# Cross-attention and mixture-of-experts block in one kernel: experts chosen first, two of four routers as VectorE dots, and the first pair of feed-forward slices in another order

## The chip, the core and the metric

The kernel runs on one core of one Trainium2 chip. The metric is the time of one execution on the device, in microseconds (us). The engines are named as in the profile: PE is TensorE's matmul (PEld its weight load), DVE is VectorE, ACT is ScalarE, POOL is GpSimd, SP is SyncE, which only issues DMAs here.

## The reference, cut to what matters

```python
x = x + xattn(layernorm(x), gate_up, ctx)        # int8-like quantised linear, silu gate, linear
x = x + ffn(layernorm(x), gate_w, w1, b1, w2, b2)

def ffn(hidden, gate_w, w1, b1, w2, b2):         # 2048 tokens, 512 wide, 8 experts, top 2
    router_logits = x @ gate_w.T                                   # [2048, 8]
    _, sel = top_k(router_logits.sum(axis=0), 2)                   # two experts for ALL tokens
    rw = softmax(router_logits[:, sel], axis=1)                    # [2048, 2]
    h = gelu(einsum('nd,kdf->knf', x, w1[sel]) + b1[sel])          # f = 2048
    y = einsum('knf,kfd->knd', h, w2[sel]) + b2[sel]
    return einsum('nk,knd->nd', rw, y)
```

The same two experts serve every token. Which two they are depends only on the sum of the logits over the tokens. The softmax over two values needs only the difference of the two logits of a token.

## The kernel before, in words

Four batches of 512 tokens are held in SBUF. The first part (the quantised layers and the second layer norm) has an order written out by hand for each engine; it ends near 140 us. The normalised tokens are transposed on PE (`normed2`), copied out by ACT and DVE, and split into a high part (`keep_hi`, ACT) and a low part (`keep_lo(b, h)`, DVE: full value minus high part), b being the batch and h one half of the 512 features. Every fp32 product is then three matmuls: high with high, high with low, low with high.

The expert choice is short: `token_sums` and `token_total` (DVE) sum the tokens, `expert_sums` (PE, four tiny matmuls) multiplies by the gate weights, `choose_experts` (DVE) takes the two largest, and SP then issues the DMAs of the chosen experts' weights (`load_w1`, `load_w2`) by register. The per-token logits come from `router(b)`: eight matmuls for each batch, an ACT copy (`keep_logits`), small transposes (`logit_columns`), and on DVE `pick_logits`; POOL takes a power (`lpow`), and `token_weights` on DVE makes the softmax weights `rw`.

The feed-forward work goes over 16 pairs p (two experts, eight slices of 256 hidden units), each in two token halves tp (batches 0 and 1, then 2 and 3). Pair 0 is done plainly: four up tiles (`plain`, 12 matmuls each), then `down` (48 matmuls), twice. From pair 1 on the up product is done by a seven-product scheme (`strassen`, 42 matmuls) over sums of operands: `last_operands`, `middle_operands`, `fourth_operand` and `operand_lo` on DVE and `operand_hi` on ACT make those sums during pair 0 and pair 1. DVE also adds every down product to the result (`outputs_of`, four instructions for each quarter; each frees one bank for PE by `y_free`), adds the bias rows (`bias_rows`) and makes the combinations `combine(e2...)` that the fourth and the later products of a pair wait for. GELU is on ACT (`gelu`), its low part on POOL (`hid_lo`), and so are the sums and low parts of the next weights (`weight_sums`, `weight_lo`, `down_lo`).

Each engine runs its own list of instructions in the written order and waits on semaphores; nothing is reordered by a scheduler. The names above are functions of kernel.py. Lines of the profile: L1291 `keep_lo`, L1295 `difference` (last and middle operands), L1310 `fourth_operand`, L1316 `operand_lo`, L1361 to L1368 `pick_logits`, L1519 to L1523 `token_weights`, L1532 `bias_rows`, L1541 `outputs_of`, L1570 `combine`, L656 `normed2`, L667 `router`, L677 `expert_sums`, L685 `logit_columns`, L850 `plain`, L805 `down`, L792 `strassen`, L340 `inv_std`, L476 `hid_lo`, L523 the power of the softmax.

Of the kernel before, what the change touches and what calls it, by code (L numbers as in the profile page):

```python
# [5 lines left out]
ALU = mybir.AluOpType  # L6
# [17 lines left out]
def xattn_ffn(  # L24
# [21 lines left out]
    NT = B * TT  # L46
    FW = 2 * P
# [14 lines left out]
    with ExitStack() as ctx:  # L62
# [6 lines left out]
        def each(name):  # L69
# [42 lines left out]
        logits = sb("logits", [2 * E, B, T])  # L112
# [8 lines left out]
        lk = sb("lk", [P, TOPK, NT])  # L121
        lmin = sb("lmin", [P, NT])
        lmax = sb("lmax", [P, NT])
# [12 lines left out]


# [16 lines left out]
        rstd = [batch_sb(f"rstd{c}_", [P, TT]) for c in (1, 2)]  # L154
        nmean = [batch_sb(f"nmean{c}_", [P, TT]) for c in (1, 2)]
# [78 lines left out]
        raw1_load, raw2_load = sem("raw1_load"), sem("raw2_load")  # L234
        b1_load, b2_load = sem("b1_load"), sem("b2_load")
# [18 lines left out]
        def _(sp):  # L254
# [63 lines left out]
        def _(pool):  # L318
# [200 lines left out]
            def first_pair():  # L519
                hid_lo(0, 0, 0)  # L520
                hid_lo(0, 0, 1)
                pool.wait_ge(lsub_ready, 1)
                g.tensor_tensor(lpow[:, :], euler[:, :], lsub[:, :], ALU.pow).then_inc(lexp_ready, 1)  # L523
                hid_lo(0, 0, 2)
                hid_lo(0, 0, 3)
                weight_sums(0)
                for i in range(4):
                    hid_lo(0, 1, i)
                for i in range(7):
                    weight_lo(0, i)  # L530
                down_lo(0, 0, 1)
                down_lo(0, 1, 0)

            first_pair()
# [6 lines left out]
        def _(pe):  # L541
# [139 lines left out]
            def logit_columns(b):  # L681
                emptied(f"r.{b}")
# [156 lines left out]
            def plain(q, n):  # L839
# [3 lines left out]
                for h in range(KD // H):  # L843
                    if q == 0:
                        pe.wait_ge(a_ops_ready, 2 * f + h + 1)
                    pe.wait_ge(lo_ready[b], h + 1)
                    hi, lo = HI_AT[s][h], LO_AT[s][h]
                    for k in range(H):
                        for a, v in ((a_hi, hi), (a_hi, lo), (a_lo, hi)):
# [5 lines left out]
            def first_pair():  # L855
                for tp in range(2):
                    pe.wait_ge(hid_ready, 8 + 8 * tp)
                    if tp == 0:
                        pe.wait_ge(drained[0], ALL_DRAINED[0])
                    plain(tp, 0)  # L860
                    plain(tp, 1)
                    if tp == 0:
                        pe.wait_ge(drained[1], ALL_DRAINED[1])
                        for b in range(B):
                            logit_columns(b)
                    plain(tp, 2)
                    pe.wait_ge(hid_ready, 8 + 8 * tp + 2)
                    plain(tp, 3)
                    if tp == 0:
                        pe.wait_ge(w2_ready, 2)  # L870
                        pe.wait_ge(drained[2], ALL_DRAINED[2])
                        pe.wait_ge(drained[3], ALL_DRAINED[3])
                    down(0, tp, 0, 0, 0, True)
                    down(0, tp, 0, 1, 1, False)
                    last = down(0, tp, 1, 2, 1, True)
                    if tp == 1:
                        last.then_inc(w2_free, 1)
                    down(0, tp, 1, 3, 0, False)
                pe.wait_ge(hid_ready, 8 + 16)

            first_pair()
# [7 lines left out]
        def _(act):  # L889
# [107 lines left out]
            def first_weights(lo, hi):  # L997
                if lo == 0:
                    act.sem_inc(hid_ready, 8)
                    act.sem_inc(e1_ready, 2)  # L1000
                    act.wait_ge(raw1_load, 16)
                for i in range(lo, hi):
                    plain_hi(i)
# [82 lines left out]
            keep_summed(2, 1)  # L1086
            keep_hi(2, 0)
            keep_hi(2, 1)
            keep_summed(3, 1)
            keep_hi(3, 0)  # L1090
            keep_hi(3, 1)
            keep_logits(0)
            keep_logits(1)
            first_weights(0, 2)
            first_weights(2, 4)
            s.activation(gelu_warm[:, :], half[:, 0:1], ACT.Gelu_apprx_tanh)
            keep_logits(2)
            keep_logits(3)
            first_down_weights()
# [6 lines left out]
            def first_pair():  # L1106
                act.wait_ge(b1_ready, 1)
                s.copy(b1_now[:, :], b1_col[:, 0:2]).then_inc(b1_ready, 1)
                act.wait_ge(b1_ready, 2)
                for tp in range(2):  # L1110
                    act.wait_ge(h_ready, 4 + 4 * tp)
                    for n in range(4):
                        act.wait_ge(prod_done, 7 * tp + n + 1)
                        gelu(0, n, TILES[n][0], TILE_BANK[n])
                    if tp == 0:
                        operand_hi(0, (T2H, T2L), 4)
                        operand_hi(0, (T3H, T3L), 4)
                        operand_hi(0, (T1H, T1L), 4)
                        operand_hi(0, (T4H, T4L), 4)
# [55 lines left out]
            first_pair()  # L1175
# [7 lines left out]
        def _(dve):  # L1183
# [172 lines left out]

            def pick_logits():
                dve.wait_ge(logcol_ps, B)
                cols = bank[3][:, 0:2 * NT * E].rearrange("p (n e) -> p n e", e=2 * E)
                for k in range(TOPK):  # L1360
                    link(v.tensor_tensor(picked[:, :, :], cols,  # L1361
                                         onehot[:, k:k + 1, :].to_broadcast([P, NT, 2 * E]), ALU.mult))
                    link(v.tensor_reduce(lk[:, k, :], picked[:, :, :], AX.X, ALU.add))
                v.tensor_tensor(lmin[:, :], lk[:, 0, :], lk[:, 1, :], ALU.min)
                link(v.tensor_tensor(lmax[:, :], lk[:, 0, :], lk[:, 1, :], ALU.max))
                v.tensor_tensor(lsub[:, :], lmin[:, :], lmax[:, :], ALU.subtract).then_inc(lsub_ready, 1)
                v.tensor_tensor(is_top[:, 0, :], lk[:, 0, :], lk[:, 1, :], ALU.is_ge)
                link(v.tensor_tensor(is_top[:, 1, :], lk[:, 1, :], lk[:, 0, :], ALU.is_ge))  # L1368
# [135 lines left out]
            choose_experts()  # L1504
            keep_lo(2, 0)
            keep_lo(2, 1)
            keep_lo(3, 0)
            keep_lo(3, 1)
            first_weights(0, 2)
            first_weights(2, 4)  # L1510
            pick_experts()
            pick_bias()
            first_down_weights()
# [112 lines left out]
```

## Time and profile before

| what | value |
|---|---|
| time, median of 3 runs | 821.65 us (820.04 to 822.15) |
| span of the profiled execution | 818.7 us |
| median of the runs less this span | 2.95 us |
| PE busy | 771.5 us, 94% of the span |
| DVE busy | 477.7 us, 58% |
| ACT busy | 354.6 us, 43% |
| POOL busy | 449.7 us, 55% |

The profile gives the span of its own execution and no time of its own around it; the median of the three runs stands 2.95 us above the span. A row of a timeline tells when an engine started an instruction, how long it was busy with it, what it reads and writes, and in brackets how long the engine was idle before it and who ended that. Instructions of one kind are merged (x4); a merged row's time runs from the first start to the last end. From about 154 us on PE is busy without a break but for fractions of a microsecond.

### The profile page before, as it was taken

To read this page: it belongs to the slowest core of one execution; us is meant where nothing else is said; L and a number is where in the kernel's file an instruction comes from. 1 tells how busy PE (TensorE), PEld (TensorE's weight loads), DVE (VectorE), ACT (ScalarE), POOL (GpSimd) and SP (SyncE) were. 2 spreads that over 40 slices of the span, in tenths; PEclk is the share of its full clock that TensorE was granted. 3 is DMA by queue.
4 is the path that set the end of the run, shared out by engine and by line. 5 is a ranking of instruction groups with operands and counts; after the bars stand their busy time and mean duration, and the time that the engine had idled before them with its cause. 6 is when DMAs were issued, how large, how long until landed. Compare 5 with 4: busy or idle time off the path is not lost.

```text
span 818.7 us, 11342 instructions
## 1 busy us (share of the span) xinstructions
PE 771.5 (94%) x3570; PEld 624.1 (76%) x3577; DVE 477.7 (58%) x669; ACT 354.6 (43%) x660; POOL 449.7 (55%) x497
## 2 busy tenths in 40 slices
PE   5688666999999999999999999999999999999998
PEld 4666455688788888888888888888888888888886
DVE  5999759797754545454545454545454545454545
ACT  3967588743442434343424343434343434242422
POOL 1789997157564646464646464646464646464622
PEclk9899968999999999999999999999999999999999
DMA  9400000301010101010101010101010101010022
GB/s 344 173 2 1 1 0 2 129 1 51 1 52 1 51 0 49 3 50 2 48 4 51 1 45 6 42 9 44 7 41 11 36 15 36 15 32 19 0 103 104
DMA packets 19077, 32.34 MB, mean 39 GB/s; under 512 B 872, under 2 KB 11240, under 8 KB 18160
## 3 DMA queue, kind: packets, MB, share of 16 engines
q1 hardware_dynamic: 18896, 31.98, 11.1%
q8 instruction: 12, 0.20, 0.1%
q10 hardware_dynamic: 160, 0.08, 0.0%
q14 instruction: 9, 0.07, 0.0%
HBM read 27.87 MB, written 4.19 MB: 39 GB/s over the span
## 4 chain that ended last, share of the span: by engine, by line
PE 83%; POOL 8%; DVE 3%; issue 2%; ACT 2%; DMA 1%; ACTq 0%; POOLq 0%; DVEq 0%
PE slot L805 42%; PE slot L792 34%; PE slot L850 3%; POOL wv L366 2%; POOL xf L383 1%; PE slot L667 1%; POOL wv L372 1%; POOL cv L366 1%; PE slot L585 1%; DVE rmax L1226 1%; DMA b_rows<-in_L_ffn_b 1%; POOL rstd L340 1%; POOL h_lo L476 1%; DVE stats L1217 1%; DVE peak_x L1226 1%
## 5 line engine op out<-in xcount | busy, mean ns | idle before, releaser
L792 PE MATMUL slot<-xo,a_hi 128*128 128x512 f32 x840 | 259.1, 390 | 0.0
L1541 DVE SCALAR_TENSOR_TENSOR res<-slot,rw,res 128x512 f32<-128x512 f32 x256 | 178.5, 750 | 130.3 <-PE slot L805 130.2
L1570 DVE TENSOR_TENSOR e<-slot,e 128x512 f32<-128x512 f32 x150 | 103.8, 692 | 173.4 <-PE slot L792 173.3
L805 PE MATMUL slot<-w_hi,h_hi 128*128 128x512 f32 x512 | 201.3, 393 | 0.4 <-POOL h_lo L476 0.4
L805 PE MATMUL slot<-w_lo,h_hi 128*128 128x512 f32 x512 | 199.6, 390 | 0.0
L805 PE MATMUL slot<-w_hi,h_lo 128*128 128x512 f32 x512 | 199.4, 390 | 0.0
L792 PEld LDWEIGHTS slot<-xo,a_hi 128*128 128x128 f32 x840 | 157.4, 188 | 33.3 <-DVE e L1570 0.2
L476 POOL TENSOR_TENSOR h_lo<-e,h_hi 128x512 fp32r<-128x512 f32 x96 | 138.1, 1451 | 55.0 <-ACT e L1104 54.0
L792 PE MATMUL slot<-xo,a_lo 128*128 128x512 f32 x420 | 163.7, 390 | 0.0
L805 PEld LDWEIGHTS slot<-w_hi,h_hi 128*128 128x128 f32 x512 | 96.1, 188 | 25.1 <-POOL h_lo L476 5.6
L476 POOL TENSOR_TENSOR h_lo<-hid,h_hi 128x512 fp32r<-128x512 f32 x32 | 44.1, 1378 | 124.7 <-ACT hid L1104 124.7
L805 PEld LDWEIGHTS slot<-w_hi,h_lo 128*128 128x128 f32 x512 | 96.2, 188 | 20.1
L805 PEld LDWEIGHTS slot<-w_lo,h_hi 128*128 128x128 f32 x512 | 96.2, 188 | 19.3
L792 PEld LDWEIGHTS slot<-xo,a_lo 128*128 128x128 f32 x420 | 78.9, 188 | 16.5
L1103 ACT ACTIVATE h_hi<-e,b_now 128x512 fp32r<-128x512 f32 x90 | 64.9, 721 | 58.0 <-DVE e L1570 57.6
L1142 ACT COPY e<-slot 128x512 f32<-128x512 f32 x30 | 17.6, 587 | 164.5 <-PE slot L792 164.5
L490 POOL TENSOR_TENSOR a_lo<-raw,a_hi 128x256 fp32r<-128x256 f32 x45 | 34.3, 761 | 95.9 <-ACT a_hi L988 95.9
L991 ACT CAST w_hi<-raw 128x512 fp32r<-128x512 f32 x32 | 19.8, 622 | 109.8 <-PE slot L805 109.8
L495 POOL TENSOR_TENSOR w_lo<-raw,w_hi 128x512 fp32r<-128x512 f32 x30 | 38.7, 1289 | 50.4 <-ACT w_hi L991 50.4
L1104 ACT ACTIVATE e<-e,b_now 128x512 f32<-128x512 f32 x90 | 63.8, 709 | 0.0
L1103 ACT ACTIVATE h_hi<-slot,b_now 128x512 fp32r<-128x512 f32 x38 | 26.2, 689 | 66.5 <-PE slot L792 56.6
L490 POOL TENSOR_TENSOR a_lo<-ssum,a_hi 128x256 fp32r<-128x256 f32 x60 | 43.7, 739 | 0.0
(145 smaller groups left out, 814.5 us busy)
## 6 DMA issues: line engine op xcount, KB each, us to landing
raw<-in_L_ffn_w SPq DMA_DIRECT2D x32, 512.0 KB, 3.4
res<-in_x SPq DMA_DIRECT2D x4, 1024.0 KB, 11.9
wv<-in_fside_BxS2xS SPq DMA_DIRECT2D x4, 1024.0 KB, 12.8
out_x<-res SPq DMA_DIRECT2D x3, 1024.0 KB, 3.9
cv<-in_ctx SPq DMA_DIRECT2D x4, 512.0 KB, 13.1
out_x<-res SPq DMA_DIRECT2D x4, 256.0 KB, 2.7
b_row<-in_L_ffn_b SPq DMA_DIRECT2D x2, 256.0 KB, 4.6
b_rows<-in_L_ffn_b ACTq DMA_DIRECT2D x1, 64.0 KB, 6.0
```

Of the source, the lines that this page charges most:

```text
L366: g.tensor_tensor(w[:, j, :], w[:, j, :], rows[b][:, 0:n], ALU.mult).then_inc(wmul_ready[b], 1)
L476: g.tensor_tensor(h_lo[:, i, :], hid[i][:, :], h_hi[:, i, :].bitcast(F32), ALU.subtract).then_inc(h_ready, 1)
L490: g.tensor_tensor(a_lo[:, i, :, :], A_OF[i], a_hi[:, i, :, :].bitcast(F32), ALU.subtract).then_inc(a_ops_ready, 1)
L495: g.tensor_tensor(w2_lo[:, f, :], raw2[:, f, :], w2_hi[:, f, :].bitcast(F32), ALU.subtract).then_inc(w2_ready, 1)
L792: last = t.matmul(dst, a[:, i, k, :], xo[tp][:, v, k, :], start=(start and n == 0), stop=(n == 3 * H - 1), skip_group_check=True)
L805: last = t.matmul(y_bank[j][:, :], a[:, i, j * P:(j + 1) * P], v[:, f, :], start=(start and n == 0), stop=(not start and n == 2), skip_gro ...
L850: last = t.matmul(TILE_BANK[n], a[:, 2 * f + h, k, :], xo[q][:, v, k, :], start=(m == 0), stop=(m == 3 * KD - 1))
L991: s.copy(w2_hi[:, f, :], raw2[:, f, :]).then_inc(w2_hi_ready, 1)
L1103: s.activation(h_hi[:, i, :], src, ACT.Gelu_apprx_tanh, bias=bias).then_inc(hid_ready, 1)
L1104: s.activation(hid[i][:, :], src, ACT.Gelu_apprx_tanh, bias=bias).then_inc(hid_ready, 1)
L1541: v.scalar_tensor_tensor(out=r, in0=y_bank[j][:, :], scalar=rw[:, ds(p, 1), n:n + 1].rearrange("p a b -> p (a b)"), in1=r, op0=ALU.mult, o ...
L1570: v.tensor_tensor(dst[:, :], src, other[:, :], ALU.add).then_inc(comb_ready, 1)
```

## The change

- The two experts' choice comes ahead of everything that can wait: on DVE `keep_lo(0, 0)` and `keep_lo(0, 1)` go behind `choose_experts`, and `expert_sums` goes ahead of both routers on PE.
- Only `router(1)` and `router(0)` stay on PE. The logit differences of batches 2 and 3 are computed on DVE by `router_dots(2)` and `router_dots(3)`: eight instructions over 128x512 with a running sum, of the tokens in SBUF and of the difference of the two gate rows, which SP loads by two DMAs more and POOL subtracts (`gate_difference`). They stand behind the outputs of the first token half.
- The softmax is done in two halves of eight columns; the denominator's `+ 1` moves to POOL (`token_power`).
- The first weight tile is loaded by two DMAs, and the first up tile starts with products of the high part alone.
- `keep_lo` of batches 2 and 3, the GELUs and the operand passes are written in another order. DVE makes the low parts of the down weights (`first_down_weights`) ahead of `keep_lo(3, 0)`, `token_weights(0)` and `keep_lo(3, 1)`.

VectorE's order behind the choice of the experts, before (`xo<-xf,xo` at L1291 is `keep_lo`, `w_lo` the down weights' low parts, `lk` the picked logits, `xf<-xf` at L1295 the operand sums):

```order
L1349 MAX_INDEX top_i<-top_v,sum_row 128x8
L1291 TENSOR_TENSOR xo<-xf,xo 128x1024 x4
L1381 TENSOR_TENSOR a_lo<-raw,a_hi 128x256 x4
L1353 CAST top_f<-top_i 128x8
...
L1388 TENSOR_TENSOR w_lo<-raw,w_hi 128x512 x2
L1361 TENSOR_TENSOR picked<-slot,onehot 128x256
...
L1295 TENSOR_TENSOR xf<-xf 128x1024 x2
```

And now, the same stretch of VectorE (`xo<-xf,xo` at L1333 is `keep_lo`, `lsub` at L1424 the logit maxima, L1574 and on the token weights):

```order
L1391 MAX_INDEX top_i<-top_v,sum_row 128x8
L1333 TENSOR_TENSOR xo<-xf,xo 128x1024 x2
L1395 CAST top_f<-top_i 128x8
...
L1438 TENSOR_TENSOR a_lo<-raw,a_hi 128x256 x4
L1333 TENSOR_TENSOR xo<-xf,xo 128x1024
L1415 TENSOR_TENSOR between<-onehot 128x16
...
L1424 SCALAR_TENSOR_TENSOR lsub<-ldiff 128x8
L1333 TENSOR_TENSOR xo<-xf,xo 128x1024
L1445 TENSOR_TENSOR w_lo<-raw,w_hi 128x512 x2
L1333 TENSOR_TENSOR xo<-xf,xo 128x1024
L1574 TENSOR_TENSOR lexp<-lpow,is_top 128x2x8
...
L1333 TENSOR_TENSOR xo<-xf,xo 128x1024
```

Six `keep_lo` passes now stand between the choice and the first operand sums, where four stood.

VectorE between the first outputs and pair 1's first combination, before (`res<-slot,rw,res` is a quarter of the outputs, L1316 `operand_lo`, L1532 the bias rows, `e<-slot,e` the first combination):

```order
L1541 SCALAR_TENSOR_TENSOR res<-slot,rw,res 128x512 x4
L1316 TENSOR_TENSOR xo<-xf,xo 128x1024 x4
L1295 TENSOR_TENSOR xf<-xf 128x1024 x2
L1310 TENSOR_TENSOR xf<-xf 128x1024
L1532 SCALAR_TENSOR_TENSOR res<-b_row,rw,res 128x512 x2
L1541 SCALAR_TENSOR_TENSOR res<-slot,rw,res 128x512 x8
L1570 TENSOR_TENSOR e<-slot,e 128x512
```

The same stretch now:

```order
L1597 SCALAR_TENSOR_TENSOR res<-slot,rw,res 128x512 x4
L1337 TENSOR_TENSOR xf<-xf 128x1024
L1405 SCALAR_TENSOR_TENSOR xf,ldot<-res,late_nmean,gate_row 128x512 x4
L1409 TENSOR_TENSOR ldiff<-ldot,late_rstd 128x4
...
L1424 SCALAR_TENSOR_TENSOR lsub<-ldiff 128x8
L1358 TENSOR_TENSOR xo<-xf,xo 128x1024 x3
L1574 TENSOR_TENSOR lexp<-lpow,is_top 128x2x8
...
L1588 SCALAR_TENSOR_TENSOR res<-b_row,rw,res 128x512 x2
L1610 TENSOR_TENSOR e<-slot,e 128x512
```

The eight dots and a second set of token weights have come in ahead of the second half's outputs, and the bias rows stand last ahead of the combination.

The diff, cut to its core:

```diff
@@ sync @@
-            load_w1(0)
+            sp.dma_start(raw1[:, 0:H, :], first[:, 0:H, :]).then_inc(raw1_top, 16)
+            sp.dma_start(raw1[:, H:KD, :], first[:, H:KD, :]).then_inc(raw1_load, 16)
             load_w2(0)
             expert.append(value_of(1))
+            for k in range(TOPK):
+                sp.dma_start(gate_row[:, k, :], gate_w[ds(expert[k], 1), :].to_broadcast([P, D])).then_inc(gate_load, 16)
@@ gpsimd @@
+            def token_power(tp):
+                pool.wait_ge(lsub_ready, tp + 1)
...
+                link(g.tensor_tensor(lpow[:, at], euler[:, at], lsub[:, at], ALU.pow))
+                g.tensor_scalar(lden[:, at], lpow[:, at], 1.0, None, ALU.add).then_inc(lexp_ready, 1)
+            hid_lo(0, 0, 0)
+            token_power(0)
+            hid_lo(0, 0, 1)
+            hid_lo(0, 0, 2)
+            hid_lo(0, 0, 3)
+            gate_difference()
+            weight_sums(0)
+            hid_lo(0, 1, 0)
+            hid_lo(0, 1, 1)
+            token_power(1)
...
@@ tensor @@
+            expert_sums()
             router(1)
-            expert_sums()
             router(0)
-            router(2)
-            router(3)
...
+            up_tile(0, 0)
+            logit_columns(1)
+            logit_columns(0)
+            up_tile(0, 1)
+            up_tile(0, 2)
+            up_tile(0, 3)
+            first_downs(0)
@@ vector @@
+            def router_dots(b):
...
+                for j in range(TT):
...
+                    ins = v.scalar_tensor_tensor(out=product, in0=res[:, n, :], scalar=nmean[1][b][:, j:j + 1],
+                                                 in1=gate_row[:, 0, :], op0=ALU.add, op1=ALU.mult,
+                                                 accum_out=ldot[:, n:n + 1])
+                link(ins)
+                link(v.tensor_tensor(ldiff[:, b * TT:b * TT + TT], ldot[:, b * TT:b * TT + TT], rstd[1][b][:, :],
+                                     ALU.mult))
...
-            keep_lo(0, 0)
+            normalise_last()
             keep_lo(1, 0)
-            normalise_last()
             token_sums(2)
-            keep_lo(1, 1)
             token_sums(3)
             token_total()
+            keep_lo(1, 1)
+            choose_experts()
+            keep_lo(0, 0)
             keep_lo(0, 1)
...
+            outputs_of(0, 0, 1)
+            middle_operands(0, 4)
+            router_dots(2)
+            router_dots(3)
+            logit_maxima(1)
+            operand_lo(0, 0)
+            operand_lo(0, 1)
+            operand_lo(0, 2)
+            token_weights(1)
+            outputs_of(0, 1, 0)
+            operand_lo(0, 3)
+            last_operands(1)
+            outputs_of(0, 1, 1)
+            fourth_operand(1)
...
+            bias_rows(0)
             pair(1, True, False)
```

## Rows read from the trace of the kernel before

**Rows 1.** The page's chain that ended last: shares by engine.

```profile
PE 83%; POOL 8%; DVE 3%; issue 2%; ACT 2%; DMA 1%; ACTq 0%; POOLq 0%; DVEq 0%
```

**Rows 2.** Timeline of PE: start us, us, instruction, idle before and its releaser.

```profile
143.41 3.14 PE L667 MATMUL slot<-xo,gwt 128*16 128x512 f32 x8
146.38 0.95 PE L677 MATMUL slot<-gwt_full,tok_total 128*128 128x8 f32 x8
147.19 6.52 PE L667 MATMUL slot<-xo,gwt 128*16 128x512 f32 x24
153.55 0.62 PE L850 MATMUL slot<-xo,a_hi 128*128 128x512 f32 x2
159.11 1.17 PE L685 MATMUL slot<-ident,logits 16*128 16x16 f32 x16
...
165.81 0.39 PE L805 MATMUL slot<-w_hi,h_hi 128*128 128x512 f32 x1
...
198.44 0.62 PE L792 MATMUL slot<-xo,a_hi 128*128 128x512 f32 x2
```

**Rows 3.** Stretches: us, PE, PEld, DVE, ACT, POOL busy, PEclk, DMA share, GB/s.

```profile
144.00:146.00 2.00, 2.00 (x7) 0.70 (x6) 1.87 (x3) 2.00 (x3) 0.00 (x0) 0.58 0.00 0
146.00:148.00 2.00, 2.00 (x15) 1.38 (x14) 1.01 (x6) 2.00 (x4) 0.00 (x0) 1.00 0.00 0
148.00:201.36 53.36, 53.15 (x243) 41.15 (x241) 45.24 (x63) 24.99 (x46) 29.67 (x22) 1.00 0.18 60
```

**Rows 4.** Timelines of POOL, SP's queue and ACT, 136 to 153 us.

```profile
136.60 1.97 POOL L340 TENSOR_TENSOR rstd<-var_e,neg_half 128x4 f32<-128x4 f32 x1
...
148.99 0.39 SPq L285 DMA_DIRECT2D raw<-in_L_ffn_w  x1
...
152.16 1.33 ACT L985 CAST a_hi<-raw 128x256 fp32r<-128x256 f32 x4 [1.87 <-DMA raw<-in_L_ffn_w]
```

**Rows 5.** Line L340 (the inverse deviations on POOL) in the whole trace.

```profile
L340 POOL TENSOR_TENSOR rstd<-var_e,neg_half x8: 1012/1033/1968, 11.8 to 136.6; 128x4 f32<-128x4 f32 x8
```

**Rows 6.** Timeline of DVE, 135 to 205 us.

```profile
145.15 0.17 DVE L1342 TENSOR_REDUCE tok_total<-tok_sum 128x4 f32<-128x16 f32 x1
...
147.86 0.16 DVE L1349 FIND_INDEX8 top_i<-top_v,sum_row 128x8 uint32<-128x8 f32 x1
147.94 4.61 DVE L1291 TENSOR_TENSOR xo<-xf,xo 128x1024 fp32r<-128x1024 f32 x4
...
160.32 0.42 DVE L1361 TENSOR_TENSOR picked<-slot,onehot 128x256 f32<-128x256 f32 x1 [2.45 <-PE slot L685]
...
162.82 2.49 DVE L1295 TENSOR_TENSOR xf<-xf 128x1024 f32<-128x1024 f32 x2
...
170.07 2.73 DVE L1541 SCALAR_TENSOR_TENSOR res<-slot,rw,res 128x512 f32<-128x512 f32 x4
...
182.41 3.45 DVE L1295 TENSOR_TENSOR xf<-xf 128x1024 f32<-128x1024 f32 x2
...
201.36 0.69 DVE L1570 TENSOR_TENSOR e<-slot,e 128x512 f32<-128x512 f32 x1 [1.97 <-PE slot L792]
...
204.49 0.69 DVE L1570 TENSOR_TENSOR e<-slot,e 128x512 f32<-128x512 f32 x1
```

**Rows 7.** Timeline of POOL, 158 to 192 us.

```profile
158.46 1.27 POOL L476 TENSOR_TENSOR h_lo<-hid,h_hi 128x512 fp32r<-128x512 f32 x1 [19.56 <-ACT hid L1104]
162.69 2.90 POOL L523 TENSOR_TENSOR lpow<-euler,lsub 128x16 f32<-128x16 f32 x1 [0.84 <-DVE lsub L1366]
...
184.74 6.21 POOL L476 TENSOR_TENSOR h_lo<-e,h_hi 128x512 fp32r<-128x512 f32 x3
```

**Rows 8.** Timelines of DVE (bias rows) and of POOL, 271 to 275 us.

```profile
271.05 0.76 DVE L1532 SCALAR_TENSOR_TENSOR res<-b_row,rw,res 128x512 f32 x1
271.96 1.54 DVE L1532 SCALAR_TENSOR_TENSOR res<-b_row,rw,res 128x512 f32 x1 [0.16 <-DVE res L1532]
...
271.50 3.16 POOL L476 TENSOR_TENSOR h_lo<-e,h_hi 128x512 fp32r<-128x512 f32 x2 [0.24 <-ACT e L1104]
```

More of the change, by code:

```diff
@@ L46, in xattn_ffn @@
     NT = B * TT
+    HALF = NT // 2
     FW = 2 * P
@@ L111, in xattn_ffn @@
         gwt_full = sb("gwt_full", [P, KD, E])
-        logits = sb("logits", [2 * E, B, T])
+        logits = sb("logits", [2 * E, 2, T])
+        gate_row = sb("gate_row", [P, TOPK, D])
+        between = sb("between", [P, 2 * E])
+        ldot = sb("ldot", [P, NT])
+        ldiff = sb("ldiff", [P, NT])
         tok_sum = sb("tok_sum", [P, KD, B])
@@ L135, in xattn_ffn @@
         b1_now = sb("b1_now", [P, 2])
+        late_rstd = [sb(f"late_rstd{b}", [P, TT]) for b in range(B)]
+        late_nmean = [sb(f"late_nmean{b}", [P, TT]) for b in range(B)]
         early = ExitStack()
@@ L853, in plain, with up_tile @@
                 last.then_inc(prod_done, 1 if n < 3 else 4)
-            def first_pair():
-                for tp in range(2):
+            def up_tile(tp, n):
+                if n == 0:
                     pe.wait_ge(hid_ready, 8 + 8 * tp)
[L858 to L866, printed above, removed]
-                    pe.wait_ge(hid_ready, 8 + 8 * tp + 2)
[L868 to L879, printed above, removed]
@@ L881, in _, with first_downs @@
-            first_pair()
+                if n == 3:
+                    pe.wait_ge(hid_ready, 8 + 8 * tp + 2)
+                if tp == 0 and n == 0:
+                    pe.wait_ge(drained[0], ALL_DRAINED[0])
+                if tp == 0 and n == 2:
+                    pe.wait_ge(drained[1], ALL_DRAINED[1])
+                plain(tp, n)
+            def first_downs(tp):
+                if tp == 0:
+                    pe.wait_ge(w2_ready, 2)
+                    pe.wait_ge(drained[2], ALL_DRAINED[2])
+                    pe.wait_ge(drained[3], ALL_DRAINED[3])
+                down(0, tp, 0, 0, 0, True)
+                down(0, tp, 0, 1, 1, False)
+                last = down(0, tp, 1, 2, 1, True)
+                if tp == 1:
+                    last.then_inc(w2_free, 1)
+                down(0, tp, 1, 3, 0, False)
@@ L882, in _ @@
+            up_tile(0, 0)
[5 more added lines that the diff above has]
+            first_downs(0)
+            for n in range(4):
+                up_tile(1, n)
+            first_downs(1)
+            pe.wait_ge(hid_ready, 8 + 16)
             pair(1, True, False)
@@ L1173, in pair @@
                         down_hi(0)
-            first_pair()
+            first_bias()
+            gelu_tile(0, 0)
+            first_down_weights()
+            keep_hi(3, 1)
+            gelu_tile(0, 1)
+            gelu_tile(0, 2)
+            gelu_tile(0, 3)
+            gelu_tile(1, 0)
+            operand_hi(0, (T2H, T2L), 4)
+            gelu_tile(1, 1)
+            operand_hi(0, (T3H, T3L), 4)
+            gelu_tile(1, 2)
+            operand_hi(0, (T1H, T1L), 4)
+            gelu_tile(1, 3)
+            operand_hi(0, (T4H, T4L), 4)
+            later_weights()
             pair(1, True, False)
@@ L1355, in pick_experts @@
                     link(v.tensor_scalar(onehot[:, k, :], iota[:, :], top_f[:, k:k + 1], None, ALU.is_equal))
-            def pick_logits():
[L1358 to L1368, printed above, removed]
+            def router_dots(b):
+                dve.wait_ge(nmr_ready[b], 2)
+                dve.wait_ge(gate_ready, 1)
+                for j in range(TT):
+                    n = b * TT + j
+                    product = part(1, (T2L, T4L)[j // 2])[:, (j % 2) * D:(j % 2) * D + D]
+                    ins = v.scalar_tensor_tensor(out=product, in0=res[:, n, :], scalar=nmean[1][b][:, j:j + 1],
[4 more added lines that the diff above has]
+                                     ALU.mult))
@@ L1596, in pair @@
                         operand_lo(1, 3)
-            first_pair()
+            first_down_weights()
+            keep_lo(3, 0)
+            token_weights(0)
+            keep_lo(3, 1)
+            last_operands(0)
+            fourth_operand(0)
+            outputs_of(0, 0, 0)
+            middle_operands(0, 3)
+            outputs_of(0, 0, 1)
[12 more added lines that the diff above has]
+            fourth_operand(1)
+            dve.wait_ge(b2_load, 16 * TOPK)
+            bias_rows(0)
             pair(1, True, False)
```

133 lines of the change are left out of this document (61 added, 72 removed), and 8 rows, old and new, of the table SLOT_USES.

## The prediction

> **What bounds the kernel now.** I read the page's chain first: PE holds 83% of it [rows 1]. Then the timeline of PE, to find from where that holds: the first plain up tile starts at 153.55 us, the first down products at 165.81, pair 1 at 198.44 [rows 2], and in between PE is busy 53.15 of 53.36 us at the full clock [rows 3]. Behind 198.44 the same work follows, untouched by the diff. So the change is worth what it moves one moment: pair 1's start on PE, together with the combination that pair 1 waits for. Third, the timeline of DVE, to see how close VectorE is behind PE there. Its first combination starts at 201.36, 2.92 us after pair 1 [rows 6], and it was PE that ended its wait. From there the two are tied: the combination's 0.69, two operand sums of 2.48 (as [rows 6] at 162.82) and the next combination from 204.49 end at about 205.2, and the sixth of the seven products, 30 matmuls of 0.227 behind 198.44, wants to start at 205.25. There is no slack. A first combination that is late by x makes PE late by x.
>
> So there are two clocks to carry through the change: when PE could reach pair 1, and when DVE gets to the first combination. The later decides.
>
> **PE's side.** VectorE no longer runs two `keep_lo` beside POOL's last inverse deviation. That took 1.97 us [rows 4] where its least is 1.01 and its median 1.03 [rows 5]: 0.94 off the path, if POOL is really left alone. `expert_sums` no longer stands behind `router(1)`: it started at 146.38 although the token total was written by 145.32 [rows 2, 6], which gives 1.06 more. The choice, done at 148.02 [rows 6], is then done at 146.0, and the first weight DMA, issued at 148.99 [rows 4], at 147.0. ACT's cast of the weights started 3.17 us behind that issue. Half the bytes can't take longer; I allow 2.4 to 3.2, so the first high part lies between 149.5 and 150.5.
>
> PE now has router(1) and router(0) from about 145.3 on, 16 matmuls. At the full clock, 24 of them took 6.52 with waits [rows 2], and back to back one takes 0.227; the granted clock was 0.58 over 144 to 146 us and 1.00 behind it [rows 3], so part of them may run at the 1.2 GHz level, at about 0.43 each. That is 3.6 to 6.9 us, an end between 148.9 and 152.2. In the new order PE also has a gap of some 1.8 us between the last transposes and `expert_sums` that the old one had not, so the clock may come back later than it did. I take 150.6, nearer the low end as the clock was back at 146 in the row. The first up tile then starts 2.95 us sooner. Half of the small transposes of the logits (1.17 us for 16, [rows 2]) go too: 0.55. PE alone could be at pair 1 3.5 us sooner, at 194.9, and the first combination could start at 197.9.
>
> The plain tile's high products first, the two DMAs and the ACT order are hidden in this: the low parts of the first weights come from DVE at about 150.9, when PE is at its fifth matmul at the soonest.
>
> **VectorE's side, as a ledger.** Before, from the choice's end at 148.02 to the first combination at 201.36 it had 53.3 us, of which 45.2 busy [rows 3] and 8.1 idle. What the change does to the busy part:
> - added, `keep_lo(0, 0)` and `keep_lo(0, 1)`, which ran ahead of the choice: 4.61 / 4 = 1.15 each [rows 6], 2.3;
> - added, eight dots over 128x512. The nearest row is the bias row, the same kind of instruction with both tensors in SBUF: 0.76 us alone [rows 8], and 0.61 to 0.68 from one start to the next where such instructions follow each other (2.73 / 4 for the outputs, [rows 6]). I take 0.65: 5.2, and 0.4 for the two small scalings. Bounds: 0.61, and 1.54, which the second bias row took beside POOL [rows 8];
> - added, the second half's maxima and token weights: 0.45 and 0.3;
> - gone, half of the picking of the logits. It ran from 160.32 to 162.79, the next instruction's start being 162.82 [rows 6]; now one product, one sum and four small ones, about 1.4. Less 1.05. The `+ 1` to POOL is worth a tenth.
>
> Sum: 45.2 + 2.3 + 5.6 + 0.75 - 1.05 = 52.8. From 146.0 on, with no wait at all, VectorE would be at the combination at 198.8. The new list has waits, though: about 1.0 for the third and fourth high part, which ACT makes behind the copy of router(0); 0.5 for the logits' columns, which stand behind PE's first tile; 0.7 for the first denominators, since POOL takes the power of 8 columns in 1.03 + 4 x 0.156 = 1.66 (between 1.03 for 4, [rows 5], and 2.90 for 16, [rows 7]) and does it behind a `hid_lo`; and 0.5 for the first down products of the second quarter. 2.7 in all, where 8.1 was idle.
>
> **POOL and VectorE beside each other.** A `hid_lo` alone takes 1.27, three in a row beside VectorE's operand sums took 6.21, and two of those sums took 3.45 where they took 2.49 at 162.82 [rows 6, 7]. So each meeting costs VectorE about 0.5 and POOL 0.8. The 45.2 hold such meetings already. New ones: two dots or so over `hid_lo` of the second half, two `keep_lo` over those of the first half, less what falls away. I put 1.1. The Trainium skill, "SBUF — State Buffer", section "Who interferes with whom", has the second of two such instructions fully blocked until the first has finished. By that rule each meeting would cost up to a whole `hid_lo` and the sum would be some 2 us more; the rows show less than half of that, and the row decides.
>
> Combination at 146.0 + 52.8 + 2.7 + 1.1 = 202.6, against 201.36: 1.2 us later. The 3.5 us that PE won are taken back in two places. The first is the third down product of pair 0, which needs banks that `outputs_of(0, 0, 0)` frees. PE is there at about 167.5 (first downs at 162.1, 24 matmuls), and VectorE, with six `keep_lo`, the token weights and three operand passes ahead, gets there at 168 to 169, so PE stands 1 to 2 us; before, the outputs started at 170.07 [rows 6], just in time for the 171.25 of then. The second is pair 1's fourth product, which waits for the combination.
>
> The profiled execution's span goes from 818.7 to 819.9 by this. The median of the runs stood 2.95 above the span, and no part of that is touched: 821.65 + 1.2 = 822.85, told as 822.9. About 0.3% (2.5 us) is what a measurement of this kernel can tell from no change, so this is no change, on the slow side.
>
> **The rivals.**
> (a) VectorE keeps up. If the waits fall together and POOL is met less often, the ledger's 52.8 start at 146.0 and end at 198.8; with the dots at 0.61 even at 198.5. PE's own limit is 197.9. Gain 2.5 to 3.5, time 818.5, taken as 3.1. For it: the old idle time was mostly VectorE waiting for PE (2.45 and 1.97 us of it at two places, [rows 6]), so it had room. Against it: 52.8 busy in 53 leaves none, and the new list interleaves with PE at three more places. 25%.
> (b) The dots are dear, and the kernel is slower. They write a running sum, which no row of VectorE shows. If that or the two SBUF tensors halve the rate, each costs 0.55 more (1024 columns take 1.24, 512 take 0.69, [rows 6]), 4.4 in all, on an engine that already decides: 1.2 + 4.4 = 5.6, time 827.2. It decides from a dot of about 0.8 us on. Against it: the bias row has two SBUF tensors and took 0.76. 13%. The Trainium skill, "Vector Engine (DVE) Microarchitecture Reference", section "7. Points that are easy to get wrong", says that this form with two SBUF sources that aren't bf16 has half the throughput, with no port left to read an accumulator back; by it the sum would be that of this rival, but the bias row contradicts the first half of it, and only the half on the accumulator is open.
> (c) The clock comes back late. If both routers and the first tile run at 1.2 GHz, the first tile starts at 152.2 and costs 12 x 0.2 more, so PE's lead is 3.5 - 1.6 - 2.4 = -0.5, and VectorE's logit columns and outputs move with it: about 2.5 later, time 824.1. For it: the gap ahead of `expert_sums`; against it: the full clock at 146 [rows 3]. 10%.
>
> **How the numbers follow.** My forecast has 52%, from 1 us sooner to 4 later by the bounds on waits, meetings and the dot. Of it 38 points are within 0.3% and 14 slower. Rival (a) gives 16 points faster and 9 within, (b) 13 slower, (c) 4 within and 6 slower. Faster 0.16, same 0.51, slower 0.33. The range takes in (a)'s 818.5 with its spread and reaches to (b)'s middle: 818.0 to 827.2.
>
> **What would show it.** Right: POOL's last inverse deviation near 1.0; the choice done near 146; first up tile near 150.6; a wait of PE of 1 to 2 us in the third down product of pair 0 with VectorE's outputs as releaser; the first combination started without idle time before it, near 202.6, and a wait of PE ahead of pair 1's fourth product. Wrong: an idle time before that combination ended by PE, at about 198 (then rival a); dots above 1.1 us each (b); a granted clock of 0.5 in the first tile (c). The whole argument fails if PE's start of pair 1 and the combination lie more than 3 us apart for another reason, such as the token weights that wait for POOL.

## The result and the profile after

The changed kernel took 830.8 us, median of 4 runs (829.21 to 831.95), against 820.99 (820.04 to 822.15) for the kernel before in the same session: 1.0126 times as long, 95% interval 1.0104 to 1.0148. By the medians it is 9.8 us slower, well outside 818.0 to 827.2; by the ratio it is 10.3. All comparisons here and below leave out three executions that took 1560 us or more.

Its timelines hold everything up to the first up tile, line by line as forecast or better: POOL's inverse deviation, the end of the choice on DVE, SP's first weight DMA, ACT's first high part, PE's first up tile. They answer to [rows 2, 4, 6].

```profile
137.33 1.00 POOL L351 TENSOR_TENSOR late_rstd<-var_e,neg_half 128x4 f32<-128x4 f32 x1
...
145.17 0.16 DVE L1391 FIND_INDEX8 top_i<-top_v,sum_row 128x8 uint32<-128x8 f32 x1
...
146.30 0.39 SPq L300 DMA_DIRECT2D raw<-in_L_ffn_w  x1
...
148.87 0.40 ACT L1015 CAST a_hi<-raw 128x256 fp32r<-128x256 f32 x1 [1.22 <-DMA raw<-in_L_ffn_w]
...
149.53 1.16 PE L873 MATMUL slot<-xo,a_hi 128*128 128x512 f32 x4 [0.79 <-ACT a_hi L1015]
```

The first tile starts 4.0 us sooner (153.55 in [rows 2]). PE then loses all of that and 10 us more before the first half of pair 1 is through. These are PE's rows: the first down product, the third down product of each half, pair 1's first matmul, pair 1's fourth product. The last column is idle time and its releaser.

```profile
161.46 0.39 PE L826 MATMUL slot<-w_hi,h_hi 128*128 128x512 f32 x1
...
170.53 0.68 PE L826 MATMUL slot<-w_hi,h_hi 128*128 128x512 f32 x1 [3.46 <-DVE res L1597]
...
195.87 0.47 PE L826 MATMUL slot<-w_hi,h_hi 128*128 128x512 f32 x1 [1.72 <-DVE res L1597]
...
201.43 0.62 PE L813 MATMUL slot<-xo,a_hi 128*128 128x512 f32 x2
...
210.49 1.22 PE L813 MATMUL slot<-xo,a_hi 128*128 128x512 f32 x2 [4.82 <-DVE e L1610]
```

Pair 1 starts at 201.43 instead of 198.44 [rows 2], and each wait names VectorE. So the next view is DVE's timeline. Shown are the largest of the pieces that are longer than the same instruction is elsewhere, a dot at its usual length, the third quarter's outputs, and the first combination.

```profile
159.51 1.26 DVE L1574 TENSOR_TENSOR lexp<-lpow,is_top 128x16 f32<-128x16 f32 x1
...
163.38 4.54 DVE L1337 TENSOR_TENSOR xf<-xf 128x1024 f32<-128x1024 f32 x2
167.96 1.63 DVE L1352 TENSOR_TENSOR xf<-xf 128x1024 f32<-128x1024 f32 x1
...
184.45 0.75 DVE L1405 SCALAR_TENSOR_TENSOR xf<-res,late_nmean,gate_row 128x512 f32<-128x512 f32 x1
...
185.13 1.78 DVE L1405 SCALAR_TENSOR_TENSOR xf<-res,late_nmean,gate_row 128x512 f32<-128x512 f32 x1
...
194.97 2.73 DVE L1597 SCALAR_TENSOR_TENSOR res<-slot,rw,res 128x512 f32<-128x512 f32 x4
...
199.34 3.99 DVE L1337 TENSOR_TENSOR xf<-xf 128x1024 f32<-128x1024 f32 x2
...
207.25 2.45 DVE L1588 SCALAR_TENSOR_TENSOR res<-b_row,rw,res 128x512 f32<-128x512 f32 x2
209.74 0.69 DVE L1610 TENSOR_TENSOR e<-slot,e 128x512 f32<-128x512 f32 x1
```

The combination starts at 209.74 with no idle time before it; it was at 201.36 [rows 6]. POOL's timeline at the same moments shows its own side of the meetings: a hidden tile's low part that takes 1.27 alone [rows 7], two more that begin with the 0.17 us instruction at 159.51, the gate difference, the weight sums, the low parts of the down weights, and pair 1's first hidden tile beside the bias rows.

```profile
155.01 2.06 POOL L487 TENSOR_TENSOR h_lo<-hid,h_hi 128x512 fp32r<-128x512 f32 x1 [16.40 <-ACT hid L1133]
...
159.46 2.53 POOL L487 TENSOR_TENSOR h_lo<-e,h_hi 128x512 fp32r<-128x512 f32 x2
...
164.58 2.27 POOL L532 TENSOR_TENSOR gate_row<-gate_row 128x512 f32<-128x512 f32 x1
166.81 1.70 POOL L492 TENSOR_TENSOR ssum<-raw 128x256 f32<-128x256 f32 x1
...
199.97 2.27 POOL L506 TENSOR_TENSOR w_lo<-raw,w_hi 128x512 fp32r<-128x512 f32 x1
...
207.11 1.26 POOL L487 TENSOR_TENSOR h_lo<-hid,h_hi 128x512 fp32r<-128x512 f32 x1 [2.63 <-ACT hid L1133]
```

Last, stretches, with columns as in [rows 3]: the whole way from the choice to the combination, PE's clock behind the two long waits, and the rest of the kernel.

```profile
145.33:209.74 64.41, 54.28 (x232) 41.60 (x229) 59.56 (x84) 26.88 (x47) 36.12 (x27) 0.96 0.20 66
170.00:172.00 2.00, 1.47 (x4) 1.22 (x5) 2.00 (x4) 0.00 (x0) 1.56 (x3) 0.66 0.00 0
172.00:174.00 2.00, 2.00 (x7) 1.52 (x6) 1.49 (x2) 0.00 (x0) 0.00 (x0) 0.50 0.00 0
...
210.00:212.00 2.00, 1.51 (x4) 1.23 (x5) 1.97 (x3) 0.00 (x0) 0.00 (x0) 0.50 0.00 0
212.00:214.00 2.00, 2.00 (x6) 1.58 (x5) 1.30 (x2) 1.14 (x2) 0.00 (x0) 0.50 0.00 0
...
229.86:818.00 588.14, 588.14 (x2582) 482.70 (x2581) 293.84 (x404) 214.53 (x401) 301.70 (x294) 1.00 0.08 27
```

DVE is busy 59.56 of 64.41 us (45.24 of 53.36 before, [rows 3]). Behind the waits of 3.46 and 4.82 the granted clock is 0.50, the 1.2 GHz level; in the kernel before it was 1.00 all the way from 148 [rows 3]. The stretch behind pair 1's first half is the same work in the same time as before (588.17 us from 219.83), so the whole loss lies ahead of it: from the first tile to there it was 66.28 us and is 80.33, 14.05 more. Four waits make 10.35 of that (the three above, and 0.35 at 221.41 for POOL), the slow clock most of the other 3.7: 8 matmuls from 170.53 and 9 from 210.49 start some 0.43 us apart instead of 0.227, which is 1.6 and 2.0 us.

### The profile page after: what moved, and what is told of

It is laid out like the page before. It is cut to its first block, busy times and chain, and to the rows that moved or that the text cites. A ratio compares the mean times of both kernels' runs of the same rounds, so it can differ in the third digit from the quotient of the medians.

```text
span 828.9 us, 11332 instructions
## 1 busy us (share of the span) xinstructions
PE 773.3 (93%) x3553; PEld 624.8 (75%) x3553; DVE 488.9 (59%) x689; ACT 353.6 (43%) x658; POOL 454.4 (55%) x501
## 3 DMA queue, kind: packets, MB, share of 16 engines
q1 hardware_dynamic: 19200, 32.51, 11.2%
## 4 chain that ended last, share of the span: by engine, by line
PE 76%; POOL 10%; DVE 6%; issue 4%; ACT 2%; DMA 1%; SPq 0%; ACTq 0%; POOLq 0%; DVEq 0%
PE slot L826 40%; PE slot L813 33%; POOL wv L377 2%; POOL h_lo L487 1%; POOL xf L394 1%; PE slot L607 1%; POOL wv L383 1%; POOL cv L377 1%; DVE rmax L1268 1%; DVE xf L1405 1%; DMA b_rows<-in_L_ffn_b 1%; POOL a_lo L501 1%; DVE xf L1337 1%; DVE res L1597 1%; DVE stats L1259 1%
## 5 line engine op out<-in xcount | busy, mean ns | idle before, releaser
L487 POOL TENSOR_TENSOR h_lo<-e,h_hi 128x512 fp32r<-128x512 f32 x96 | 135.6, 1425 | 63.1 <-ACT e L1133 62.0
L506 POOL TENSOR_TENSOR w_lo<-raw,w_hi 128x512 fp32r<-128x512 f32 x30 | 40.6, 1353 | 48.6 <-ACT w_hi L1021 48.5
```

What stands on the lines that cost most here:

```text
L487: g.tensor_tensor(h_lo[:, i, :], hid[i][:, :], h_hi[:, i, :].bitcast(F32), ALU.subtract).then_inc(h_ready, 1)
L506: g.tensor_tensor(w2_lo[:, f, :], raw2[:, f, :], w2_hi[:, f, :].bitcast(F32), ALU.subtract).then_inc(w2_ready, 1)
```

## The experiments

Every comparison has 5 rounds and at least 5 runs of the kernel tested; intervals are 95%. The kernel before took 820.1, 819.4 and 819.8 us in the three sessions. The changed kernel itself ran in none of them, so what an edit gives back is told as the difference of two ratios to the kernel before. By their two intervals such a difference is good to 2 to 2.6 us (an estimate).

**Is it the meetings of POOL and VectorE?** GpSimd's work for pair 0 becomes fills of the same places, in the changed kernel and in the one before (the edit cut, without its semaphores):

```diff
 def hid_lo(p, b, i):
+    if p == 0: g.memset(h_lo[:, i, :], 0.0); return
 ...            # the same in weight_sums, weight_lo and down_lo
-    g.tensor_tensor(gate_row[:, 0, :], gate_row[:, 0, :], gate_row[:, 1, :], ALU.subtract)
+    g.memset(gate_row[:, 0, :], 0.01)
```

> The changed kernel with POOL's instructions of pair 0 (low parts, weight sums, gate difference) turned into fills of the same tiles: as many, in the same places and with the same semaphores, but reading nothing; so what they compute is left out. The two powers stay. Meeting theory: of VectorE's 59.6 busy us between the choice and the first combination 5 to 7 were waits inside its instructions beside POOL; they go, operand sums are back at 1.24 each, the combination comes at 202 to 204 instead of 209.7, PE's waits shrink below 3 us each and the clock stays up: 6 to 9 us less than the changed kernel, ratio 1.001 to 1.005. Rival, VectorE's own added work is the cost: under 2 us less.

> The same fills in the kernel before (pair 0's low parts and weight sums left out). There PE never waits in this stretch, so what VectorE gains is idle time: ratio 0.999 to 1.001. If the kernel gets faster by more than 1 us, PE was held by meetings there too, and my reading that PE alone decided before is wrong.

Measured: 819.11 us, 0.999 (0.9979 to 1.0002), for the changed one; 818.88, 0.9992 (0.9977 to 1.0007), for the one before. The whole loss goes, some 11 us where 6 to 9 were expected, and the kernel before doesn't notice: it was bound by PE. The same stretch, from the choice to the combination, with POOL silent, of the changed kernel:

```profile
145.00:198.16 53.16, 51.99 (x232) 40.69 (x229) 46.39 (x86) 25.82 (x46) 14.85 (x26) 1.00 0.24 80
```

and of the kernel before:

```profile
148.93:202.32 53.39, 53.16 (x243) 41.02 (x241) 39.15 (x62) 25.23 (x46) 11.04 (x22) 1.00 0.18 61
```

This prices the meetings. In the changed kernel they cost VectorE 59.56 - 46.39 = 13.2 us; in the kernel before 45.2 [rows 3] - 39.15 = 6.1. The instructions themselves grew from 39.15 to 46.39. The fills are also shorter than what they replace, so a POOL that merely came late could be a rival. The changed kernel's rows are against it: none of VectorE's idle times over 0.3 us in that stretch ended with POOL, nor did such a wait of PE's before 221.41, and VectorE's idle time didn't fall without the meetings (4.85 us with, 6.77 without). On DVE's timeline of the silenced kernel the long pieces are short again, and the combination comes at 198.16:

```profile
157.78 0.17 DVE L1586 TENSOR_TENSOR lexp<-lpow,is_top 128x16 f32<-128x16 f32 x1
...
159.64 2.48 DVE L1349 TENSOR_TENSOR xf<-xf 128x1024 f32<-128x1024 f32 x2
162.15 1.22 DVE L1364 TENSOR_TENSOR xf<-xf 128x1024 f32<-128x1024 f32 x1
...
196.59 1.54 DVE L1600 SCALAR_TENSOR_TENSOR res<-b_row,rw,res 128x512 f32<-128x512 f32 x2
198.16 0.69 DVE L1622 TENSOR_TENSOR e<-slot,e 128x512 f32<-128x512 f32 x1
```

**Which meetings?** The same edit split in two: the hidden tiles' low parts, the sums and the gate difference as fills; or the weights' low parts alone.

> The changed kernel, in which GpSimd's low parts of the hidden tiles of pair 0, its weight sums and its gate difference are memsets of the same places (these results are left out), and its low parts of pair 1's weights are computed as in the changed kernel. Theory (meetings of GpSimd and VectorE hold the loss, most of them between 155 and 195 us): the pair of operand sums at 163 falls from 4.54 to about 2.5 us, the first wait of TensorE in the first down products falls below 1 us, and the median is 822 to 825, of the 11.7 us that silencing all of it gave back. Rival (the late meetings, with the low parts of the weights at 196 to 205 us, are what delays the combination, since those ahead of them lie in slack): 827 to 830.

> The changed kernel, in which GpSimd's low parts of pair 1's first weights and of its down weights are memsets (results left out), and all that GpSimd does for pair 0's hidden tiles is computed. Theory: only what VectorE does between 196 us and the combination gets shorter, the pair of sums from 3.99 to about 2.5, operand_lo from 1.80 to 1.2 and one or two more, 2 to 4 us together: median 827 to 829, first wait of TensorE unchanged at 3.4 us. Rival: 822 to 825.

Measured: 823.15 us, 1.0038 (1.0025 to 1.0051), and 825.65 us, 1.0073 (1.0053 to 1.0094). Against 1.0126 that is 7.2 and 4.3 us, together about the 11.2 of silencing both. So both groups count, and within the noise they add up. The theory was right on the first. The second lies between its 827 to 829 and the rival's 822 to 825. One row that it had not counted is the two bias rows right ahead of the combination, 2.45 us above and 1.54 here. What they met in the changed kernel is pair 1's first hidden tile at 207.11, which here begins at 205.18, behind the combination at 204.82. With the hidden tiles silent PE had no first wait at all, and still waited 4.04 us for the combination.

**Is it the dots?** In the changed kernel two small copies take the place of the eight dots, with the logit differences left out; in the kernel before, eight instructions of that kind and size (tokens times tokens, into scratch) stand behind the second outputs. The first edit, cut:

```diff
-v.scalar_tensor_tensor(out=product, in0=res[:, n, :], scalar=nmean[1][b][:, j:j + 1],
-                       in1=gate_row[:, 0, :], op0=ALU.add, op1=ALU.mult, accum_out=ldot[:, n:n + 1])   # x8
+v.tensor_copy(ldot[:, b * TT:b * TT + TT], nmean[1][b][:, :])                                            # x2
```

> The changed kernel with the eight dots left out (two small copies stand in; the router weights of batches 2 and 3 are not computed). VectorE theory: it decides pair 1's start, so its list gets shorter by 8 x 0.675 = 5.4 us and the late combination (209.7) comes near 203.5. PE's wait of 4.8 us ahead of pair 1's fourth product then goes, and with it the stretch at the half clock behind it: 6 to 9 us less than the changed kernel, a ratio to before of 1.001 to 1.005. Rival, POOL and VectorE meeting: the time left out is only exchanged for other meetings, the gain stays under 3 us (ratio 1.009). Rival, the first half (wait of 3.5 us at 170) decides alone: no gain at all, ratio 1.012.

> The kernel before with eight instructions added on VectorE behind the outputs of the first half's second quarter, of the same kind and size as the dots (tokens times tokens with a running sum, into scratch), 5.4 us of work; nothing uses them. No-slack theory: VectorE's idle time behind that place was 2.3 + 2.0 us, so the first combination comes 1 to 3 us later and the kernel with it: ratio 1.001 to 1.004, and more if meetings with POOL are added. Rival, the dots are harmless and the order of the rest cost the time: ratio 1.000.

Measured: 827.57 us, 1.0087 (1.0067 to 1.0107), and 830.21 us, 1.012 (1.0098 to 1.0141). Both main expectations missed. Without the dots only 3.2 us come back, near the first rival's "under 3". VectorE then waited 2.00, 1.14 and 1.23 us for ACT's high parts ahead of `operand_lo`, and its combination was at 205.32, 4.4 sooner, not 6. Nor did PE's wait ahead of pair 1's fourth product go: it was 4.82, as in the changed kernel. With the dots the kernel before lost 10 us, not 1 to 3. Its timelines, DVE first, then PE, and PE's stretch:

```profile
182.78 0.74 DVE L1561 SCALAR_TENSOR_TENSOR xf<-res,neg_half 128x512 f32<-128x512 f32 x1
183.45 1.77 DVE L1561 SCALAR_TENSOR_TENSOR xf<-res,neg_half 128x512 f32<-128x512 f32 x1
185.26 6.83 DVE L1317 TENSOR_TENSOR xo<-xf,xo 128x1024 fp32r<-128x1024 f32 x4
...
199.39 2.73 DVE L1542 SCALAR_TENSOR_TENSOR res<-slot,rw,res 128x512 f32<-128x512 f32 x4
...
200.28 0.77 PE L806 MATMUL slot<-w_hi,h_hi 128*128 128x512 f32 x1 [7.41 <-DVE res L1542]
```

```profile
200.00:204.00 4.00, 3.72 (x9) 3.00 (x10) 2.11 (x4) 0.00 (x0) 0.62 (x1) 0.50 0.42 131
```

Eight instructions 0.675 us apart are 5.4 us. The outputs behind them are 7.9 late (191.53 without them): two dots took 1.77 each, and four `operand_lo`, pushed over POOL's work, 6.83, where the kernel before has, with as many columns, this row, followed without a gap up to the outputs:

```profile
177.87 4.62 DVE L1316 TENSOR_TENSOR xo<-xf,xo 128x1024 fp32r<-128x1024 f32 x4
...
191.53 2.73 DVE L1541 SCALAR_TENSOR_TENSOR res<-slot,rw,res 128x512 f32<-128x512 f32 x4
```

PE waits 7.41 of it and then runs at half clock. So there was no room on VectorE at that place to begin with.

Why 4.82 stays: the outputs of the third quarter free the banks that PE goes on with, and from there PE is at its fourth product in 9.8 us (195.87 to 205.67). VectorE, from the start of the same outputs to the combination, needs 14.8 in the changed kernel (194.97 to 209.74) and as much without the dots (190.47 to 205.32). What lies ahead of those outputs moves both engines alike. In the kernel before it was 9.8 us (191.53 to 201.36), since the last `operand_lo`, three operand sums and the bias rows stood ahead of them. The change put these behind, and meetings add about 3: with the weights silent the same piece takes 11.75 us, and PE's wait is 1.83.

**POOL held back.** The gate difference and the weight sums wait until both first outputs are done, so that they no longer meet the operand sums.

```diff
+pool.wait_ge(y_free, 2 * TT)
 gate_difference()
```

> The changed kernel with one wait on POOL: the gate difference and the sums of the next weights (5 instructions) start only when VectorE has done the first outputs. Nothing is taken away. Meeting theory: the two operand sums and the third (4.54 and 1.63 us in the changed kernel, 2.49 and 1.24 alone) get back to their own times, the first outputs start at about 167.2 instead of 169.6, PE's wait of 3.5 us at 170 shrinks to about 1 and the clock does not fall behind it: 2 to 4 us less than the changed kernel, ratio to before 1.007 to 1.010. Rival, VectorE's own work alone counts: nothing changes, ratio 1.0126.

Measured: 828.35 us, 1.0095 (1.0072 to 1.0118), 2.5 us less, inside the expected 2 to 4, though the two intervals overlap. The signs came only in part. The sums took 3.58 us, not 2.49, as a hidden tile's low part was still beside them. PE's first wait fell from 3.46 to 2.04, not to 1, the granted clock behind it did fall to 0.50, and the 4.82 stayed.

**What does the clock add?** The fourth up tile of the first half is computed twice, which puts 12 matmuls into the place of the first wait.

```diff
+if tp == 0 and n == 3:
+    plain(tp, n, False)
 plain(tp, n)
```

> The changed kernel with PE computing the fourth up tile of the first half twice: 12 matmuls, 2.7 us more work on PE ahead of the first down products. VectorE theory: PE waits for VectorE 3.5 us at 170, so the added work goes into that wait: within 0.5 us of the changed kernel, or up to 1.5 less if the shorter wait keeps the clock up. Rival, PE decides: 2.7 us more (ratio 1.016).

Measured: 828.02 us, 1.0091 (1.0072 to 1.011). More work on PE made the kernel 2.9 us faster, barely clear of the noise. No theory had that size. The changed kernel behind its first wait (above) spaced 8 matmuls 0.43 instead of 0.227 us, 1.6 us of slow clock, and the second outputs waited for them. Here the wait is gone, and this is the clock in its place:

```profile
168.00:172.00 4.00, 4.00 (x19) 3.34 (x18) 3.96 (x6) 0.00 (x0) 3.92 (x5) 1.00 0.00 0
172.00:176.00 4.00, 4.00 (x19) 3.30 (x19) 3.25 (x6) 0.00 (x0) 1.07 (x1) 1.00 0.00 0
```

Part of the gain is not the clock: the two operand sums took 2.48 in this run, as POOL's work fell elsewhere. The rows split it. From the choice to the combination VectorE is 2.2 us faster here (62.25 for 64.41). Of that 1.0 is there when the first outputs start, 23.28 us behind the choice for 24.30, so it comes from the sums. The rest comes behind them, from the clock and the wait that is gone. It also warns of the run before this one: here, with POOL not held, the first outputs start as soon behind the choice as there with POOL held (23.20 us), so what holding POOL gave can't be told from where the meetings happen to fall.

**Can the change be saved?** `fourth_operand(1)`, the bias rows and the middle operands move behind pair 1's combinations, and ACT's `operand_hi(1)` behind the gelus; then that with POOL held as above; then that with the tile computed twice.

```diff
-    if first and tp == 0:
-        middle_operands(1, 3)
-        middle_operands(1, 4)
 ...
+        fourth_operand(1)          # behind the last combination
+        middle_operands(1, 3)
+        middle_operands(1, 4)
 ...
+        bias_rows(0)               # behind those of the second half
 ...
-fourth_operand(1)                  # ahead of pair 1
 ...
-bias_rows(0)
```

> The changed kernel with VectorE relieved ahead of pair 1's first combination: the fourth operand sum of the second half (1.2 us) and pair 0's bias rows (2.5) go behind pair 1's combinations, and the two middle operand sums (2.5) leave the gap between its first and second combination; ACT makes the second half's high parts behind the GELUs. Same work, other place. Theory: the combination stood 14.8 us behind the start of the third quarter's outputs, now 11.1; PE's wait of 4.8 becomes about 1.1, the half clock behind it goes: 5 to 7 us less than the changed kernel, ratio 1.004 to 1.007. Rival, the wait moves on into the second half of pair 1, where VectorE now has 20 us of work in 20.4: under 2 us gained.

> Both: POOL's gate difference and weight sums held until the first outputs (that alone gave ratio 1.0095), and VectorE relieved as in the kernel above. If the two add up, 8 to 10 us less than the changed kernel: ratio 1.000 to 1.003. A version that beats the kernel before would need PE's other waits (1.7 and 2.0 us) gone too.

> The changed kernel with both reliefs of f2_relieved_held (later VectorE work moved behind the first combinations, GpSimd's gate difference and weight sums held until the first outputs) and, as in e3_tile_twice, the fourth up tile of the first half computed twice (12 matmuls more, 2.7 us). Theory (a wait of about 3 us costs TensorE its clock on top of itself, so work in its place is free and saves that): the wait in the first down products goes, the granted clock stays at 1.00 there, and the median is 823 to 825, at or under the 825.3 of f2_relieved_held. Rival (work is work): 826.5 to 828.

Measured: 826.72 us, 1.0087 (1.0066 to 1.0108); 825.27, 1.0069 (1.0049 to 1.0089); 825.86, 1.0075 (1.0059 to 1.0092). The first two gave 3.2 and 4.7 us where 5 to 7 and 8 to 10 were expected. The combination came at 205.01 and 203.41, and PE's wait for it fell to 1.09 and 1.05 as meant. But in the first the waits of 3.19 and 1.69 us ahead of it stayed, with the slow clock behind the 3.19, and both have new waits of 1.2 to 1.3 us at two places behind it. In the second the longest waits of PE were 1.76 and 2.23 and the clock was 1.00 throughout, so doubling the tile had no clock to give back. It missed its 823 to 825, and "work is work" missed too: 2.7 us of matmuls more changed nothing measurable. No version with all its work beat the kernel before.

## Why the prediction was wrong

**Right, or better than said.** POOL's inverse deviation (1.00 us), the choice (145.33 for 146.0), the first tile (149.53 for 150.6), and a granted clock of 1.00 over 144 to 152 us. PE's lead was 4.0 us at the first tile for 2.95, and 4.35 at the first down product (161.46) for 3.5. Rival (c) is out. VectorE decides, through the two places named, the third down product and the combination, which started with no idle time before it, and through one not named, the third quarter's outputs (1.72 us). Rival (a) is out too. One slip bears on nothing: a first issue at 147.0 and 2.4 to 3.2 us make 149.4 to 150.2 for the first high part, not 149.5 to 150.5.

**The dots.** 0.75 us each, 0.675 apart, for the 0.65 that I took. The running sum costs a read of 0.08 us that lies inside this spacing. Rival (b) is out as priced. And the half of its rule in the Trainium skill, "Vector Engine (DVE) Microarchitecture Reference", section "7. Points that are easy to get wrong", that was still open isn't borne out: with two fp32 tensors in SBUF and an accumulator the trace shows no halving. The time that rival (b) gave, 827.2, was nearer to the result than mine, for another reason.

**The step that failed** is the term of meetings, "POOL and VectorE beside each other", put at 1.1 us; it measured 13.2 - 6.1 = 7.1. The ledger against the runs: start of the choice -0.7; VectorE's own work, 52.8 less the 6.1 of meetings that it inherited, 46.7 against 46.39 measured, -0.3; idle time 4.85 for 2.7, +2.1; meetings 13.2 against 6.1 + 1.1, +6.0. These make 7.1, and 202.6 + 7.1 = 209.7 is where the combination started. The instructions were counted well; their company was not.

I went wrong in two ways there. First the price of one: I took 0.5 us from 3.45 for two sums. But only one of those two had met POOL: the first ended after 1.25 us, the second took 2.20. So did the sum behind them, and the two bias rows took 3.37. Alone these are 1.23 and 1.54. These are rows of the kernel before:

```profile
185.89 2.20 DVE L1310 TENSOR_TENSOR xf<-xf 128x1024 f32<-128x1024 f32 x1
188.13 3.37 DVE L1532 SCALAR_TENSOR_TENSOR res<-b_row,rw,res 128x512 f32<-128x512 f32 x2
```

In the changed kernel small instructions of 0.17 took 1.26, a dot 1.78 for 0.75, two sums 4.54 for 2.49. So a full meeting costs VectorE about 1 us, up to a whole 128x512 instruction of POOL. The Trainium skill, "SBUF — State Buffer", section "Who interferes with whom", says that the second of two such instructions is blocked until the first is done. These rows agree: the instruction of 0.17 us at 159.51 ended at 160.77, and the low part that POOL began at 159.46 takes 1.27 alone, to 160.73. I had weighed that rule and put it aside for an average over two sums of which one had met nothing.

Second the number of meetings. With 1.1 us at 0.5 each I had two new ones; at 1 us each the 7.1 are some seven (an estimate), so the count is the larger part of the error. I counted those of the added instructions. But everything behind the dots moves onto POOL's work for the second half, the old instructions too, as the four `operand_lo` of e4_before_dots show. That a denser list leaves POOL fewer gaps to fall into (8.1 us of idle time before, 4.85 now) is argued, not shown by itself.

**A term was missing**: what a wait of PE costs beyond itself. I had a stall of 1 to 2 us; it was 3.46, then 4.82 in front of pair 1's fourth product, and behind both the granted clock was at its lower level for about 4 us. That is the 1.6 and 2.0 us above. The 2.0 lie behind the combination, and so the combination is 8.4 us later and the kernel some 10. Nor did one sum up to the combination show that VectorE's list must also be short enough between two of PE's releases: the 14.8 us behind the third quarter's outputs, 9.8 before, are what the wait of 4.82 comes from.

## What to carry to other kernels

Before work is put on VectorE to spare another engine, compare its busy time with GpSimd silenced and with it running: the difference, here 6.1 of 45.2 us, is not a constant, and here it doubled. Price a meeting by the worst row of the trace, not by the mean of several. Where two engines wait for each other at several places, add up VectorE's list between each two of them, and not only the whole. And take a wait of TensorE of some us in the middle of the kernel as more than its length, since the clock may drop behind it.

## What the runs showed that was not expected

GpSimd's fills don't meet VectorE: with as many instructions in POOL's list (26 for 27) and 14.85 us busy, the long pieces on DVE up to the combination were gone. POOL's power of 8 columns took 2.08 and 2.59 us, where 1.66 was worked out from [rows 5, 7]. VectorE was busy beside it both times; that this held it up is likely and was not tried.

Whether PE's clock falls behind a wait does not go by the length of the wait alone in these runs. It fell behind waits of 3.19, 3.46, 4.04, 4.82 and 7.41 us, and behind one of 1.83 and one of 2.04; it did not behind others of 2.23, 2.56 and 3.42. In every case it was back at 1.00 some 3.5 to 6 us later. What decides between these was not tried.
